# Fused pair-mix and blur kernel: x1's statistics one unit sooner, and the filter's steps moved up on all engines

## The reference, cut to what matters

```python
def reference(x, Wa, ba, Wb, bb, Wg, bg, Wo, bo, filt):     # x: (2, 64, 64, 64) float32
    # _gn: normalise over 32 groups of 2 channels, eps 1e-5
    p = _gn(x)
    a, b = p @ Wa + ba, p @ Wb + bb
    g = sigmoid(p @ Wg + bg)
    x = x + (g * einsum('bijk,bikl->bijl', a, b)) @ Wo + bo      # "x1"
    # depthwise 4x4 filter on the image dilated by 2, stride 2: four taps reach each pixel
    return x + conv(_gn(x), filt)
```

## Time and profile before

| quantity | us |
|---|---|
| median of 3 runs | 62.74 (62.19 to 62.99) |
| the profiled execution, its own time | 62.93 |
| its span, first to last instruction | 61.0 |
| POOL / DVE / PE / ACT busy in the span | 38.0 / 41.5 / 48.2 / 29.3 |

### The profile page before, as it was taken

One profiled execution on the slowest core, in us unless ns is written; L12 is line 12 of the kernel. 1 busy time (PEld: TensorE's weight loads), 2 busy tenths in 40 slices (PEclk: granted clock), 3 DMA queues, 4 the chain that ended last, 5 costly groups with the idle time before them and its releaser, 6 DMA issues.

```text
span 61.0 us, 2458 instructions
## 1 busy us (share of the span) xinstructions
PE 48.2 (79%) x1038; PEld 36.6 (60%) x1038; DVE 41.5 (68%) x111; ACT 29.3 (48%) x56; POOL 38.0 (62%) x51
## 2 busy tenths in 40 slices
PE   3999989998997985979999976998789899940000
PEld 3998878664865964756986735975468756400000
DVE  1073578888865679627479895479879978999200
ACT  5400005124494140784339999248892708990000
POOL 1000035809999599997281876984882997899500
PEclk9999999999999999999999999999999999999755
DMA  0899993000000000000000004031004004000494
GB/s 0 215 326 307 322 393 134 0 11 0 0 11 0 0 11 0 0 0 16 0 0 11 0 0 172 11 119 63 0 5 172 8 3 172 5 0 0 172 350 165
DMA packets 2604, 4.84 MB, mean 79 GB/s; under 512 B 289, under 2 KB 417, under 8 KB 2593
## 3 DMA queue, kind: packets, MB, share of 16 engines
q1 hardware_dynamic: 2592, 4.69, 22.4%
HBM read 2.59 MB, written 2.10 MB: 77 GB/s over the span
## 4 chain that ended last, share of the span: by engine, by line
PE 32%; POOL 24%; DVE 10%; issue 8%; ACT 4%; POOLq 2%; DVEq 0%
POOL y L253 11%; PE ps_ot L608 6%; PE ps_ab L641 6%; POOL rstd L218 6%; PE ps_ag L629 5%; POOL gn L240 5%; PE ps_ot L681 4%; PE ps_ag L653 2%; DVE y L468 2%; DVE bsb L445 2%; ACT gate L315 2%; PE ps_ab L665 2%; POOLq L55 2%; DVE part L414 2%; ACT rt L302 2%
## 5 line engine op out<-in xcount | busy, mean ns | idle before, releaser
L253 POOL TENSOR_TENSOR y<-y,prod 128x512 f32<-128x512 f32 x11 | 14.0, 1273 | 5.0 <-DVE y L468 4.6
L218 POOL TENSOR_TENSOR rstd<-veps,half 128x2 f32<-128x2 f32 (+1 forms) x7 | 5.7, 819 | 11.1 <-DVE veps L438 11.1
L583 PE MATMUL ps_ab<-zeros 128*128 128x128 f32 x54 | 9.3, 337 | 1.0 <-DVE zeros L486 1.0
L247 POOL TENSOR_TENSOR xb<-xs,par 128x512 f32<-128x512 f32 x8 | 8.5, 1098 | 1.6 <-issue 1.6
L583 PEld LDWEIGHTS ps_ab<-zeros 128*128 128x128 f32 x54 | 8.5, 244 | 1.0 <-DVE zeros L486 1.0
L315 ACT ACTIVATE gate<-ps_ag,par 128x512 f32<-128x512 f32 x8 | 5.5, 687 | 7.4 <-PE ps_ag L653 7.4
L302 ACT ACTIVATE rt<-ps_ot 128x512 f32<-128x512 f32 x7 | 4.0, 593 | 10.0 <-PE ps_ot L608 10.0
L345 ACT ACTIVATE prod<-x,coef 128x512 f32<-128x512 f32 x11 | 7.6, 711 | 0.0
L308 ACT ACTIVATE at<-ps_ag,par 128x512 f32<-128x512 f32 x8 | 5.5, 686 | 4.2 <-PE ps_ag L629 4.1
L454 DVE TENSOR_TENSOR zt<-ps_ab,gate 128x512 f32<-128x512 f32 x8 | 5.5, 684 | 2.8 <-ACT gate L315 2.3
L410 DVE BATCH_NORM_STATS2 part<-xs 128x6 f32<-128x512 f32 x8 | 5.4, 683 | 2.5 <-DMA xs<-x 2.5
(11 more groups left out here) (59 smaller groups left out, 71.4 us busy)
## 6 DMA issues: line engine op xcount, KB each, us to landing
xs<-x SPq DMA_DIRECT2D x8, 256.0 KB, 5.3
out<-y SPq DMA_DIRECT2D x8, 256.0 KB, 2.0
par<-params SPq DMA_DIRECT2D x1, 353.0 KB, 5.4
par<-params SPq DMA_DIRECT2D x1, 128.0 KB, 4.0
```

The costliest lines, as they stand in the source:

```text
L218: nc.gpsimd.tensor_tensor(job_of(rstd, job), job_of(veps, job), half[:, 0:columns(job)], ALU.pow).then_inc(rstd_done, 1)
L247: nc.gpsimd.tensor_tensor(xb[:, w, b, :, :], xs[:, w, b, :, :], bo.broadcast_to([128, ROWS, D]), ALU.add).then_inc(xb_ready, 1)
L253: return nc.gpsimd.tensor_tensor(y[:, w, b, :, :], y[:, w, b, :, :], prod[:, n % 2, k, :, :], ALU.add)
L583: nc.tensor.matmul(bank[:, 0:128], zeros[:], zeros[:], start=True, stop=True)
```

## The change

Nothing is added or taken out of the arithmetic; the lists of the engines are reordered. On DVE, job 2's `deviation` and `variance` move from unit 2 into unit 1, around `z_out(1)`. x1's jobs 3, 4 and 5 move up: the parts of wave 0 and the aggregate into unit 2, its deviation and variance into unit 3, job 4's into unit 5, and job 5's deviation ahead of the last `x1_out`. `filter_right(w - 2, 0)` moves from the end of an even unit to directly behind `b_out`, ahead of both `x1_out`. At the end `filter_right(2, 0)` moves from behind `variance(6)` to ahead of `deviation(6)`. PE's statistics products and `halo` follow. On POOL `add_bo(2)` goes behind both `normalise`, wave 1's coefficients and base ahead of `add_products(0, 1)`, wave 2's ahead of the last addition of (1, 1), and wave 3's coefficients behind `add_products(2, 0)`. On ACT `mean_column`, `halo_row`, `filter_base1` and the first product go ahead of `gate_out` in even units; `filter_base1` gets one wait more; `halo_row(3)` goes behind `filter_base1(2)`. One of two idle products ahead of the last `product_o` goes.

```diff
@@ gpsimd
             add_bo(1)
-            add_bo(2)
             inverse_root(2)
             pool.wait_ge(rstd_done, 3)
             normalise(2)
             normalise(3)
+            add_bo(2)
             add_bo(3)
...
             filter_coefs(0)
             filter_base(0)
             add_products(0, 0)
-            add_products(0, 1)
             filter_coefs(1)
             filter_base(1)
+            add_products(0, 1)
             add_products(1, 0)
-            add_products(1, 1)
+            pool.wait_ge(right_ready, 4)
+            link(add_product(1, 1, 0))
             filter_coefs(2)
             filter_base(2)
+            add_product(1, 1, 1).then_inc(add_done, 1)
+            add_products(2, 0)
             filter_coefs(LAST)
-            add_products(2, 0)
             pool.wait_ge(right_ready, 6)
             add_product(2, 1, 0).then_inc(add_done, 1)
@@ scalar
             def filter_base1(w):
                 act.wait_ge(coef_ready, w + 1)
+                act.wait_ge(halo_ready, w + 1)
...
                 if n == 0:
                     a_out(g)
                     if w >= 2:
+                        mean_column(w - 2)
                         halo_row(w - 2)
-                        mean_column(w - 2)
+                        filter_base1(w - 2)
+                        filter_product(w - 2, 0, 0)
                     gate_out(g)
                     if w >= 2:
-                        filter_product(w - 2, 0, 0)
+                        filter_product(w - 2, 0, 1)
                 else:
...
                     a_out(g)
                     if w >= 2:
-                        filter_product(w - 2, 0, 1)
+                        filter_product(w - 2, 1, 0)
...
                     gate_out(g)
                     if w >= 2:
-                        filter_base1(w - 2)
-                        filter_product(w - 2, 1, 0)
                         filter_product(w - 2, 1, 1)
+            mean_column(LAST - 1)
             halo_row(LAST - 1)
-            mean_column(LAST - 1)
...
+            filter_product(LAST - 1, 0, 0)
             mean_column(LAST)
-            filter_product(LAST - 1, 0, 0)
-            halo_row(LAST)
             filter_product(LAST - 1, 0, 1)
             filter_base1(LAST - 1)
+            halo_row(LAST)
@@ vector
                     aggregate(2)
+                    deviation(2)
+                    z_out(1)
+                    variance(2)
                     dve.wait_ge(params_in, 16)
                     nc.vector.tensor_reduce(tsum[:], ftap[:, :, 1:4:2, 1:4:2], mybir.AxisListType.XY,
                                             ALU.add).then_inc(tsum_ready, 1)
-                    z_out(1)
                 elif n == 0:
-                    job = 2 if g == 2 else X1JOB + w - 2
-                    deviation(job)
-                    variance(job)
                     b_out(g)
+                    if w >= 2:
+                        filter_right(w - 2, 0)
                     x1_out(w - 1, 0)
                     x1_out(w - 1, 1)
                     z_out(g)
-                    if w >= 2:
-                        filter_right(w - 2, 0)
+                    x1_part(w - 1, 0)
+                    if w == 1:
+                        x1_part(w - 1, 1)
+                        aggregate(X1JOB)
                 else:
-                    if w == 1:
-                        x1_part(w - 1, 0)
-                        x1_part(w - 1, 1)
                     b_out(g)
                     if w > 1:
-                        x1_part(w - 1, 0)
+                        x1_part(w - 1, 1)
+                        aggregate(X1JOB + w - 1)
+                    if w < LAST:
+                        deviation(X1JOB + w - 1)
+                    z_out(g)
                     if w == LAST:
-                        z_out(g)
-                    if w > 1:
-                        x1_part(w - 1, 1)
-                    aggregate(X1JOB + w - 1)
-                    if w < LAST:
-                        z_out(g)
-                    if w >= 2:
+                        filter_right(w - 2, 1)
+                        deviation(X1JOB + w - 1)
+                    else:
+                        variance(X1JOB + w - 1)
+                    if w == 2:
                         filter_right(w - 2, 1)
             job = X1JOB + LAST
             x1_out(LAST, 0)
-            deviation(job - 1)
             x1_out(LAST, 1)
             variance(job - 1)
             x1_part(LAST, 0)
             x1_part(LAST, 1)
             aggregate(job)
+            filter_right(LAST - 1, 0)
             deviation(job)
...
             variance(job)
-            filter_right(LAST - 1, 0)
@@ tensor
                 elif n == 0:
-                    job = 2 if g == 2 else X1JOB + w - 2
                     product_a(g)
-                    stat_product(job, 0)
-                    if w >= 2:
-                        halo(w - 2)
+                    if w == 2:
+                        halo(0)
+                    elif w == LAST:
+                        stat_product(X1JOB + 1, 1)
                     product_b(g)
-                    stat_product(job, 1)
+                    if w == LAST:
+                        halo(1)
                     product_o(w - 1)
...
                 product_g(g)
+                if g == 1:
+                    stat_product(2, 0)
+                elif g == 3:
+                    stat_product(X1JOB, 0)
                 product_ab(g)
-            idle_products(2, ps_ot[:, 0, :])
+                if g == 1:
+                    stat_product(2, 1)
+                elif g == 3:
+                    stat_product(X1JOB, 1)
+                elif n == 1:
+                    stat_product(X1JOB + w - 1, 0)
+            idle_products(1, ps_ot[:, 0, :])
             product_o(LAST)
-            stat_product(X1JOB + LAST - 1, 0)
+            stat_product(X1JOB + LAST - 1, 1)
             halo(LAST - 1)
-            stat_product(X1JOB + LAST - 1, 1)
```

## The result

The changed kernel takes 66.68 us (median of 4 runs, 66.41 to 66.89), the kernel before 62.69 (4 runs, 62.19 to 62.99): 1.064 times as long, 95% interval 1.056 to 1.073. The forecast was 63.2, with a range of 61.9 to 64.6 and a chance of 0.23 for "slower". The prediction was wrong. In all ratios with an interval a few longer executions of the same kernels are left out.

What follows compares the result with a forecast made beforehand. POOL's last addition with the stores behind it, and DVE's nearly equal end, bound the kernel; steps from -1.24 up to z_out(3) to -1.06 at the last store sum to +0.41 on 62.93, stated as 63.2 us, range 61.9 to 64.6.

Steps and rivals of the forecast that it cites:

- Unit 1: Job 2's statistics sooner on DVE and PE: z_out(3) at 26.28 instead of 27.52, a gain of 1.24 us.
- POOL's list as the limit for wave 0's base: POOL up to unit 4: its list lets wave 0's base end at 31.51 instead of 32.31, only 0.8 us sooner.
- the loss of the unit 1 gain by DVE's wait in unit 4: Unit 4: DVE stands 2.5 us ahead of filter_right(0, 0) for wave 0's base; x1_out(1, 0) comes 1.21 us later.
- The deviation ahead of `z_out(5)`: Unit 5 on DVE: aggregate, exchange and deviation come first, z_out(5) at 37.39 instead of 35.81; step of +0.37 us.
- DVE's wait ahead of `filter_right(2, 0)`: Near the end: DVE waits 0.85 us for wave 2's base; deviation(6) at 51.81 instead of 50.46, +1.35.
- ACT's late `halo_row(3)`: At the end, behind one product and filter_base1(2) on ACT: last_tap(3) at 54.0 instead of 52.53; step of +0.12 us.
- rival 2: Unit 4: PE's 2.6 us without work lowers TensorE's clock, unit 5 costs 2.1 us more: 65.4 us, chance 0.12.
- the rows speak against it, though not by much: Argument against a clock fall in unit 4: after the last matmul the clock fell only after more than 3 us idle.
- I walk the new lists with the old durations: Method for the whole kernel: reordered lists summed with each instruction's length from the old trace.
- The 0.67 of a `filter_right`: Units 4, 6 and the end: each filter step on DVE was charged 0.67 us.
- DVE's +1.47 at its end: End of DVE's list: all work from last_tap(3) on shifts by +1.47, ending at 58.37 instead of 56.90.
- +0.41 at the last store: End of the span: POOL's last addition ends at 57.66 instead of 57.25, so the span goes from 61.0 to 61.4.

Runs made afterwards that it cites:

- the two missing effects taken away on the chip: Changed kernel with POOL waiting for filter_right(1, 0) and (2, 0) before the additions behind its bases, plus eight idle products in unit 4: 63.37 us, ratio 1.010.
- the idle products: Changed kernel with eight idle products on PE behind product_ab(4), in the gap of unit 4: 65.39 us.
- the waits: Changed kernel with POOL waiting for filter_right(1, 0) before add_products(0, 1) and for filter_right(2, 0) before the last addition of (1, 1): 64.97 us.
- the kernel with the old end: Changed kernel with filter_right(2, 0) behind variance(6), halo_row(3) ahead of the second product, wave 3's coefficients ahead of add_products(2, 0): 63.75 us.

## Why the prediction was wrong, point by point

**What held.** Unit 1 (`z_out(3)` at -1.24, measured -1.09 on the shifted scale). POOL's list as the limit for wave 0's base, and the loss of the unit 1 gain by DVE's wait in unit 4 (`z_out(4)` within 0.07 us). The deviation ahead of `z_out(5)`, DVE's wait ahead of `filter_right(2, 0)`, ACT's late `halo_row(3)`. With the two missing effects taken away on the chip, the kernel runs in 63.37 us, where the forecast said 63.2.

**First failed step: the chance and the reading of rival 2.** The mechanism, its place and nearly its price stood there; the step that failed is "the rows speak against it, though not by much". I took the clock at the end of the trace, where it stayed up for about 3 us after the last matmul, as a sign that a gap of 2.6 us is safe. That one observation bounds nothing: in the middle of the kernels the clock fell behind gaps of 2.62, 2.45, 2.30, 1.97, 1.89 and 1.76 us, and near the end of two of them behind 1.06 and 1.07. The longest gap that I had seen it survive was 0.99 us, and the new one was beyond that. The Trainium skill's rule that activity releases the throttle ("TensorE: Matmul & The Clock Gate", Part 1) agrees with the two traces: 0.50 behind 2.30 us without work, 1.00 with the idle products in their place. It is no certain loss either: in the changed kernel the clock stayed at 1.00 through gaps of 1.18 us (ahead of 45.77) and 2.06 us (ahead of 56.04). The price was 1.29 us by the idle products, against the 2.1 that I gave, as the first transposes and `product_a` still ran at the full clock (0.63 and 0.67) and `product_ab` saw the end of the slow stretch (0.82).

**Second failed step: "I walk the new lists with the old durations".** The 0.67 of a `filter_right` was measured where POOL stood idle or made small operations. The change moves POOL's additions of two SBUF tiles directly ahead of two of the three, which are then held until the addition has ended. Each cost 1.0 us, and together they cost 1.71 (the waits). I gave it neither a term nor a rival. The trace before had one sign of it, the other way round: POOL's inverse root, begun while `filter_right(2, 0)` ran (51.86 to 52.61), took 1.15 us where its like takes 0.71.

```profile
52.03 1.15 POOL L218 TENSOR_TENSOR rstd<-veps,half 128x2 f32<-128x2 f32 x1 [0.37 <-DVE veps L438]
```

The Trainium skill, "GPSIMD Engine Reference", section 1, lists the SBUF interfaces as shared with VectorE, with contention for DVE instructions with two SBUF inputs. The trace agrees: of DVE's instructions beside POOL's additions, line 486 (one SBUF tile, one in PSUM) kept its 0.75 us at 57.61, and line 471 took 1.74.

**The end.** I forecast that DVE's +1.47 at its end would shrink to +0.41 at the last store, because the three stores were bunched. That held in part in the kernel with both effects taken away: +1.06 at DVE's end, +0.4 at the span's end (61.4). In the changed kernel DVE's end is so late that it is the bound: 61.99, and 3.1 us on to the span's end.

**What stays open.** When a gap lets the clock fall. The same gap near the end left it up in the changed kernel (2.06 us) and had it fall in two others (2.05 us), and the kernel with the old end had the hole in its clock in some executions and seemingly not in others, with the same instructions. This was not followed.

## What to carry to other kernels

A step put ahead of others on an in-order engine must be ready when the engine arrives: ask which list delivers its input, and walk that list before the gain. When instructions change neighbours, check durations by pairs and not only one by one: what POOL will be doing when a VectorE instruction with two SBUF tiles starts, and what becomes of TensorE's clock in the gap that opens. Look also at the clock of the whole kernel after each change: a fall at another place alters what the change seems to be worth. The move of the statistics was good (61.77 us, and 62.00 with job 2's alone) and the move of the filter bad; tried as one change, the second hid the first.

## What the runs showed of the hardware that I had not expected

- A VectorE `scalar_tensor_tensor` of 128x512 float32 with two tiles in SBUF takes 0.75 us alone. Started while a POOL instruction on 128x512 SBUF tiles ran, it ended 0.54 to 0.55 us after that instruction, in all ten cases (0.82 to 1.76 us long): it was held, not slowed. One-input POOL operations did it too (0.97). In turn POOL's next instruction took 1.60 instead of 1.28 us, and 1.05 where its like took 0.62. VectorE's instructions with one operand in PSUM kept 0.75.
- TensorE's granted clock went from 2.4 to 1.2 GHz about 1.1 us after the end of a 2.30 us gap, in the midst of dense matmuls, and was back at 37.9 us; in another kernel it went down within a gap of 2.05 us, and in the changed kernel it stayed up through one of 2.06. After the last matmul of the kernel before it had stayed up for about 3 us, after that of the changed kernel for 2.2.
